# Max passes of a graph network: scan in place in PSUM, carried column first, ring slot freed by the copy of the landed rows

## The reference, cut to what matters

```python
def _gin_layer(h, src, dst, W, b):
    msgs = h[src]
    agg = jax.ops.segment_max(msgs, dst, num_segments=N_NODES)
    agg = jnp.where(jnp.isfinite(agg), agg, jnp.zeros_like(agg))
    return (h + agg) @ W + b
```

## Time and profile before

| | us |
|---|---|
| median of the runs | 6546.63 |
| span of the profiled execution | 6562.2 |
| first max pass, PE's first pick to the carry | about 4385 to 5430 |
| second max pass | about 5495 to 6500 |

### The profile page before, as it was taken

The page is one execution under the profiler, slowest core; times in us unless marked ns, Lnnn a source line. Parts: engine busy times, 40 slices in busy tenths (PEclk is TensorE's granted clock), DMA queues, the critical chain, the costliest instruction groups (busy, mean ns, idle before and its releaser), DMA issues.

```text
span 6562.2 us, 44574 instructions
## 1 busy us (share of the span) xinstructions
PE 2310.6 (35%) x14635; PEld 1387.8 (21%) x14635; DVE 4507.3 (69%) x5353; ACT 2519.0 (38%) x3136; POOL 3944.3 (60%) x3878
## 2 busy tenths in 40 slices
PE   4988400000020000000100000046877783778886
PEld 2775300000000000000000000023444441444443
DVE  7978587777767777776787777764655653656654
ACT  2330144444424444443344444433444442444443
POOL 1001377777747777775677777656665555566664
PEclk8998755555555555555555555567888895889887
DMA  2233354444434444443454444412333322333332
GB/s 64 83 136 135 110 163 152 153 147 146 152 117 151 157 148 147 152 148 113 134 160 152 147 148 146 142 46 86 102 110 101 101 95 73 102 110 109 98 103 84
DMA packets 257146, 807.72 MB, mean 123 GB/s; under 512 B 72026, under 2 KB 108938, under 8 KB 253123
## 3 DMA queue, kind: packets, MB, share of 16 engines
q0 software_dynamic: 162688, 416.67, 22.2%
q1 hardware_dynamic: 94279, 389.14, 16.2%
HBM read 473.23 MB, written 332.30 MB: 123 GB/s over the span
## 4 chain that ended last, share of the span: by engine, by line
POOL 38%; PE 26%; issue 22%; DVE 8%; ACT 2%; another core or an unknown queue 2%; DMA 1%; SPq 0%; DVEq 0%; POOLq 0%; ACTq 0%
POOL arena L2316 38%; PE pair_ps L1864 20%; PE pair_ps L1966 3%; DVE outs L917 2%; ACT outs L1702 1%; PE banks_ps L1830 1%; PE banks_ps L1942 1%; DVE outs L995 1%; PE pair_ps L1873 0%; DVE bn_st L700 0%; DVE H L1048 0%; ACT arena L1680 0%; PE pair_ps L1982 0%; PE banks_ps L1807 0%
## 5 line engine op out<-in xcount | busy, mean ns | idle before, releaser
L2316 POOL DMA_INDIRECT arena<-table,src_i x3596 | 3684.6, 1025 | 1549.8 <-issue 1134.4
L1842 PE MATMUL pair_ps<-ident,tails 128*128 128x128 f32 x9 | 2.7, 439 | 3331.7 <-DVE tails L1246 3331.7
L1864 PE MATMUL pair_ps<-bias,arena 128*128 128x384 bf16 x4050 | 803.9, 348 | 279.9 <-issue 239.9
L1092 DVE TENSOR_TENSOR pair_ps<-pair_ps,arena 128x1792 f32<-128x1792 f32 x168 | 341.5, 2033 | 764.7 <-DMA arena<-table,src_i 589.1
L1864 PE MATMUL pair_ps<-work,arena 128*128 128x384 bf16 x4050 | 760.5, 338 | 206.4 <-issue 204.8
L995 DVE TENSOR_TENSOR_SCAN outs<-arena,banks_ps 128x1920 f32<-128x1920 f32 x112 | 465.2, 4153 | 494.3 <-ACT banks_ps L1688 446.2
L1842 PEld LDWEIGHTS pair_ps<-ident,tails 128*128 128x128 f32 x9 | 1.5, 213 | 3334.0 <-DVE tails L1246 3334.0
L1140 DVE TENSOR_TENSOR_SCAN work<-work,banks_ps 128x1920 f32<-128x1920 f32 x168 | 697.7, 4153 | 5.8
L1562 ACT ACTIVATE LD<-DE 128x112 f32<-128x112 f32 x168 | 49.8, 296 | 1440.9 <-issue 571.3
L1864 PEld LDWEIGHTS pair_ps<-bias,arena 128*128 128x128 bf16 x4050 | 406.9, 102 | 661.6 <-issue 452.8
L1582 ACT COPY outs<-work 128x1792 f32<-128x1792 f32 x171 | 541.0, 3165 | 0.0
(11 more groups left out here) (321 smaller groups left out, 4353.4 us busy)
## 6 DMA issues: line engine op xcount, KB each, us to landing
rows_att<-outs SPq DMA_DIRECT2D x165, 1008.0 KB
rows_plain<-outs SPq DMA_DIRECT2D x110, 896.0 KB
arena<-table,src_i POOLq DMA_INDIRECT x3596
kept_counts<-arena SPq DMA_DIRECT2D x15, 2000.0 KB, 6.4
bias<-sources SPq DMA_DIRECT2D x108, 192.0 KB
arena<-kept_counts SPq DMA_DIRECT2D x10, 2000.0 KB, 8.3
outs<-kept_counts SPq DMA_DIRECT2D x5, 2000.0 KB, 8.0
table<-arena SPq DMA_DIRECT2D x18, 512.0 KB, 3.0
```

The lines of the kernel that those rows point to most:

```text
L1092: chain(v.tensor_tensor(prod, prod, ring[:, s, :, 0:D], ALU.mult))
L1864: ins = pe.matmul(picked_ps[g % 2], parts3[:, a, t, :], hots_made[g % 2][:, :, t, :], start=t == a == 0, stop=t == NB - 1 and a == 2)
L2316: pool.indirect_dma_start(dst, None, tab, bass.IndirectOffsetOnAxis(ap=idx, axis=0))\
```

## The change

The scan writes its output over its input, `msg`, in PSUM, and `sums_plain` in SBUF goes. `lay_sums` therefore reads `msg`. The carried column is copied from `msg` to `msg` ahead of the flags and has a semaphore of its own, `s_first`. The copy of the landed rows waits for it and for the group's `lay_sums`, and signals `s_taken`, for which POOL's ring now waits. The copy of PE's rows signals `s_spread`, which now counts only the groups that have such rows. PE's transposes wait for the scan (`s_agg`) of the group two before theirs.

```diff
 def plain_group(k, g):
-    v.wait_ge(s_spread, scanned(k, g))
-    v.tensor_tensor_scan(sums_plain, decay_plain, msg, 0.0, ALU.add, ALU.max).then_inc(s_agg, 1)
+    if picks(k, g):
+        v.wait_ge(s_spread, made_group(k, g) + 1)
+    else:
+        v.wait_ge(s_taken, scanned(k, g))
+    v.tensor_tensor_scan(msg, decay_plain, msg, 0.0, ALU.add, ALU.max).then_inc(s_agg, 1)
...
 # ACT, run_pass
     if g < GROUPS:
+        act.copy(column(msg, 0), column(msg, GROUP) if g else zero_bf[:, 0:D]).then_inc(s_first, 1)
         act.copy(decay_plain..., flags[:, g, :]...)
         act.wait_ge(s_land[g % RING], landed(k, g))
+        if g:
+            act.wait_ge(s_rows, rows_base[k] + g)
+        act.wait_ge(s_first, scanned(k, g))
         landed_to = GROUP - picks(k, g)
-        act.copy(by_edge(msg)[:, 0:landed_to, :], ring_plain[:, g % RING, 0:landed_to, :])
+        act.copy(by_edge(msg)[:, 0:landed_to, :], ring_plain[:, g % RING, 0:landed_to, :])\
+            .then_inc(s_taken, 1)
         if picks(k, g):
             act.wait_ge(s_upright, made_group(k, g) + 1)
-            act.copy(by_edge(msg)[:, landed_to:GROUP, :], upright_ps[g % 2])
-        act.copy(column(msg, 0), column(sums_plain, GROUP) if g else zero_bf[:, 0:D])\
-            .then_inc(s_spread, 1)
+            act.copy(by_edge(msg)[:, landed_to:GROUP, :], upright_ps[g % 2]).then_inc(s_spread, 1)
...
 # ACT, lay_sums
-        act.copy(out_plain[:, j0:j1, :], by_edge(sums_plain)[:, j0:j1, :]).then_inc(s_rows, 1)
+        act.copy(out_plain[:, j0:j1, :], by_edge(msg)[:, j0:j1, :]).then_inc(s_rows, 1)
...
 # PE, turn_picked
-    await_count(s_spread, scanned(k, g - 2), 2, it)
+    await_count(s_agg, scanned(k, g - 2), 2, it)
...
 # POOL, run_pass
             if g >= RING:
-                pool.wait_ge(s_spread, scanned(k, g - RING))
+                pool.wait_ge(s_taken, scanned(k, g - RING))
```

More of the change, by code:

```diff
@@ L224, in gnn_kernel @@
         out_plain = outs[:, 0:GROUP * D].rearrange("p (j w) -> p j w", j=GROUP)
-        sums_plain = outs[:, GROUP * D:(2 * GROUP + 1) * D]
         out_att = outs[:, :].rearrange("p (s j w) -> p s j w", s=OUT, j=GROUP)
@@ L486, in gnn_kernel @@
         s_agg = sem("agg_groups")
-        s_spread = sem("rows_spread")
+        s_spread = sem("picked_rows_spread")
+        s_taken = sem("landed_rows_spread")
+        s_first = sem("sums_carried_on")
         s_att = sem("att_steps")
```

## The result

The changed kernel takes 6899.44 us (median of 4 runs, 6893.86 to 6923.68), beside 6545.56 for the kernel before on the same chip (4 runs): ratio 1.0549, 95% interval 1.0517 to 1.0581. It is 5.5% slower. The profiled span is 6922.0 us against 6562.2, a difference of 359.8.

A forecast was written before the change was run, and what follows sets the result against it. The max passes were taken as bound by a ring of waits, long POOL gather trains holding PE's results. Steady part +276, pass starts +27.6, other parts 0: 6546.6 + 304 = 6850 us, 4.6% slower; own range 6700 to 7050, whole 6380 to 7130.

The forecast's parts named there:

- part 4: POOL's release moves 6.1 us earlier, to the landed copy's end; gather trains join and hold PE: +276 and +27.6 us.
- The pair: Steady max passes: two groups share a train of 22 gathers, intervals 11.2 and 30.2 us, 41.4 together, 20.7 each.
- release lag: ACT's copy of PE's turned rows starts 2.96 us after a train's last gather; 2.15 instead takes 40 us off.
- three intervals without gathers: Last three of a pass's 53 scan intervals, without gathers: 33.5 us in all, at 11.2 each.
- rival A: Trains merge worse, PE's remaining picks running after the train at halved clock: 24.0 us a group, 7185 us; chance 0.10.
- part 2: ACT's sums copy reading PSUM at a 15-element step: taken as 3.3 us, bounds 1.65 and 3.31, possibly 1 us slower.
- Part 1: Scan in place in PSUM: no change from 4.15 us, bounds -0.1 to +0.1 us a scan.
- Part 3: Carry copy ahead of the flags: scan starts about 0.4 us sooner, left inside the uncertainty; added waits cost 0.
- The start of a pass: POOL runs on with eleven more gathers, so PE's rows come 13.8 us later; 27.6 us for both passes.
- The signs named: Expected profile: trains of 22 or more, pauses of 13 us or more, ACT waits to 18 us, lower clock.
- Rival B: Early release removes a real POOL wait, faster: 6290 us, or 6140; milder form 6425, intervals near 16.6; chance 0.26.
- Rival C: No change: new long trains replace old ones one for one, mean stays 17.6 us; 6547 within 33 us; chance 0.12.

The follow-up runs named there:

- e1: Changed kernel, but POOL's slot release again waits for the copy of PE's rows, as before: 6518.05 us against 6530.9, ratio 0.9981.
- e2: Kernel before with the early release alone, the landed-rows copy signalling POOL: 6951.06 us, ratio 1.0657.
- e4: e1 plus a wait before each train's seventh gather for PE's finished pick two groups back: 6439.35 us, ratio 0.9864.
- e8: Kernel before with only the cut of e4, a wait for PE's pick after six gathers: 6406.07 us, ratio 0.9763.
- e3: Changed kernel with each max-pass gather fetching 128 bytes a row instead of 512, same number of gathers: 6897.76 us.
- e6: e1 plus six memsets of unused memory on POOL behind each group's eleven gathers: 6365.55 us against 6563.55.
- e9: e1 plus three memsets on POOL behind each train, where e6 had six: 6517.02 us, ratio 0.9965.
- e5: Changed kernel with PE's picks in two parts instead of three, 50 matmuls a group and not 75: 6734.93 us.

## Why the prediction was right

**The size and the sign** came out: 6850 forecast, 6899.44 measured, inside the forecast's own range. The decisive step was part 4, read from the earlier trace rows; by e1 the loss goes with the early release, and by e2 it comes with it alone.

**The pair.** 22 gathers, intervals of 11.2 and 30.2, 41.4 together; measured 13.1 and 28.5, 41.6, with a train of 22. The near agreement is in part luck, from errors of opposite sign: the release lag was 0.35 us after the train in place of 2.96, and in the short interval the transposes came 12.0 us after the scan (5183.59) and not 8.7. In other trains of 22 the lag goes up to 3.8 us. The plain pairs average 42.4 us in the first pass and 41.6 in the second.

**The mis-sized term** is that every two groups form a pair. The three intervals without gathers took 34.1 us in the first pass (predicted 33.5), the other 50 took 21.35 and 21.15 us and not 20.7. That is 55 us for both passes, of the 55.8 by which the two profiled spans differ from the forecast (the medians: 49). About half the groups (more in the second pass) run in threes behind trains of 33, at 21.7 us each, and these 51 groups account for some 50 of the 55 us. The threes are rival A in a milder form: PE's pick is itself held, and L1696 comes 10.6 us after the train's end (the rival had 9.65 and 24.0 us a group). My reason against A, that the second transposes are due before PE is held, failed because the landed copy, and so the release, comes 9.0 and not 10.6 us after a scan: a second release falls inside the train more easily than I had it.

**That 9.0** is the term of part 2. I took 3.3 us for the sums copy, by its nearest row in shape, and it is 1.65, the lower bound of the range. The Trainium skill, SBUF — State Buffer, section "Door 1: The DMA port swizzle", gives PSUM lines of 8 bytes against 16 in SBUF, by which a 60-byte step would cost in PSUM as much as in SBUF; the measured 1.65 us, the time of the copy of as many elements in L1604, speaks against that for this read, and the measurement decides. A faster copy, off the path, made the release earlier and the trains longer: e2, with the slow copy, has 4 trains of 33 and not 17. But it is not what made the result slower than forecast, since e2 is slower still; there the pairs themselves take 42.9 us.

**Part 1** is right: 4162 ns for 4153. **Part 3**: the scan does start sooner after the copy of PE's rows (0.50 us after L1696, not 0.79), but the 0.4 us a group that I left inside the uncertainty are not there as a gain. e1, with parts 1 to 3 and the old release, is 13 us faster, 0.12 us a group, and its commonest interval is 17.0 and not 16.7. The ring there runs over POOL's train, of which the scan is no part.

**The start of a pass**: +13.8 each, measured +9.9 and +15.7, together 25.5 for 27.6.

**The signs named**: the clock lower and POOL's wait at the landed copy were seen. Trains of 22 or more are the rule, with five of 11 among them. Of the 22 pauses after the first train of the first pass 15 are of 13 us or more (up to 20.5), the others 2.1 to 12.1. ACT's longest wait at the turned rows is 27.4 us past the start, beyond the 18 that pairs alone give.

**Rival B** is refuted as an account of the release: POOL's 197 us of waiting were no slack. The time and interval of its milder form, 6425 us and near 16.6, come of the opposite edit, a wait added to POOL's train (e4: 6439, e8: 6406); that is chance. **Rival C** fell: new long trains did not replace the old ones one for one.

## What to carry to other kernels

Where a profile puts a wait between two engines down to no releaser ("remote", "issue") and its end lies at the end of another engine's burst, treat the burst as the cause: find out how long the engine can be shut out, and what breaks the burst up, before removing a wait. A wait that looks like lost time on the busy engine can be what lets the other one through; here one more wait in the middle of a train gained 1.4 to 2.4%, and one let go earlier cost 5.5%. A buffer released earlier is no gain when the engine that fills it already has its work ahead.

## What the runs showed of the hardware

- A train of indirect gathers on POOL holds back PE's results: 17 matmuls on record in 48 us of it, at granted 0.50 (1.2 GHz of 2.4). Rows of a quarter of the size do it as well (e3: 6898 against 6899 us). Memsets on POOL do not, and with gaps of 2.8 us after every eleven gathers no engine waits for the rest of the hold (e6), with granted clock 0.94 and 0.95 in its max passes against 0.85 and 0.87. Gaps of 1.6 us did not do it (e9), and gaps of 3.0 us alone do not either. The Trainium skill, SBUF — State Buffer, section "Who interferes with whom", says that DMA never contends with a compute engine; for the bytes moved e3 agrees, and the hold by their issue is not told there.
- A gather that is issued while DVE builds one-hots without a gap waits for them: 5139.89 and 5180.79 above take 3.9 and 2.9 us and end 0.8 us after DVE's fifteenth, in e5 one takes 6.5. The Trainium skill, same section, has a DVE instruction with two SBUF inputs contend with a GpSimd instruction that reads SBUF, but infers that tensor_tensor leaves the descriptor generation of a DMA alone. The one-hots are tensor_tensor with two SBUF inputs, so these rows agree with the first and speak against the second. From 4385 us on the changed kernel has 35 gathers over 1.4 us with 77 us of extra time, against 13 with 44 us before: a smaller matter, and no account of PE's hold.
- ACT reads 1792 floats at a 60-byte step in 1.65 us from PSUM and in 3.3 us from SBUF.
- A scan of 1920 elements that writes over its input in PSUM takes 4162 ns, one that writes SBUF 4153.
